# First transposes issued between the row loads, 24 tiles of row statistics moved to the second and third batch, slot rows fetched a slot earlier

## The chip, the cores and the metric

The kernel runs on one core of a Trainium2 chip. The metric is the device time of one execution in microseconds (us); lower is better. The engines are TensorE (PE, with its weight loads listed apart as PEld), VectorE (DVE), ScalarE (ACT), GpSimd (POOL) and SyncE (SP, which here only issues DMAs and waits).

## What is computed

Two layers over x [16, 256, 256] with a context ctx of the same shape and a mask of keys:

```python
x = x + _L0_xattn_ref(ctx_1024, ctx_1024, _layernorm(x, axis=-1), mask, W_out, b_out)   # 16 heads of 16
x = x + _L0_ffn_ref(_layernorm(x, axis=-1), w1, b1, w2, b2)                             # quantised MLP
x = x + _L1_xattn_ref(_layernorm(x, axis=-1), ctx_1024, ctx_1024, Wq, bq, ...)          # autocorrelation
x = x + _L1_ffn_ref(_layernorm(x, axis=-1), Wfc_s, ..., Wr, Wfc, bfc, Wproj, bproj)     # 8 experts, top 2, and a shared one
```

The first line is a softmax attention: the layer-normed x are the queries, ctx is both keys and values, masked scores are -1e20, and the result is projected by W_out. The layer norm of a row needs its mean and variance ("row statistics"). The last line routes each of the 4096 rows to 2 of 8 experts and adds the gated results to the output of the shared expert.

## The kernel before

The 4096 rows are 32 tiles of 128; tile T sits in `X[:, T, :]`, two tiles (`NQ`) are one batch. The program runs four blocks: `attention`, `quant_mlp`, `autocorrelation`, `moe`. In each, every engine has its own program text in hand-written order, and semaphores tie them together.

**attention** works in phases `B` from -2 to 16 (`PHASES`), each of 8 steps `hp` (a pair of heads). In phase B, PE computes the scores of batch B+1 (`scores`, L569), which DVE reduces to row maxima with the mask added (`take_max`, L747, four 256-column calls in a step), and the transposed scores of batch B (`scoresT`, L582), which ACT exponentiates (`exponent`, L479). PE then weighs the values (`weigh`, L615), transposes and projects. PE may write the scores of the next step only when DVE has read those of the step before (`s_red`), and `scoresT` of a step only when the exponent two steps back is done (`s_exp`).

Ahead of that, batch b+2 is prepared in phase B = b. DVE reads the mask (`see_mask`). POOL combines the rows' scale with it (`set_live`), ACT normalises the two tiles (`normal_rows`, L460), and POOL splits the result in f16 parts (`split_q`, L394 to L397) and the context rows too (`split_k`, L383 to L386). Then SP turns them by DMA transposes of 128 rows each (`turn_k` L297, `turn_q` L307, `turn_mask` L317). POOL also adds the projection's bias to the rows of x (`add_bias`, L402), which waits for all of x, `bo_bc` and `woT` (`s_x[2]` at 80), copies the values (`values`), and cuts expert weights for the last block in f16 parts (`cut_piece`, L151 to L155, two pieces in a phase). The first `scores` of all, in phase -1, wait for `turn_k(0)` and `turn_q(0)`.

Row statistics are taken in three groups of tiles (`GROUPS`): 2, 6 and 24 tiles. For each group DVE runs `measure` (one `bn_stats` a tile, L693) and `norm_begin` (6 small steps), ACT the square root (`std`, L453), DVE `norm_end` (6 more). Group 2, the 24 tiles from batch 4 on, is first used by `set_live(4)`, in phase 2. Exponent and square root are in different tables of ACT, so a switch is an ACT_TABLE_LOAD.

**moe** runs the shared expert over 16 chunks and then 39 slots of 256 rows (every sixth, from slot 2 on, has 128). A tick of PE is: transpose the rows of slot s+1 (`rows_T`, L2028), first layer of slot s (L2043), second layer of slot s-1 (L2056). SP fetches for each slot the first weights (`first_weights`, L1835, 1 MB, once the hidden layer of slot s-2 has left PSUM), the second weights (`second_weights`, L1842, 1 MB, once DVE has taken the output of slot s-2) and the rows (`slot_rows`, L1851, once PE, POOL and DVE have used those of slot s-2, since there are two row buffers). All three stand in one queue. POOL copies the rows' owners (`own`, L1900) and adds the gated output rows to the output in DRAM (`add_rows`, L1908), one slot after the other, each waiting for the landing of the one before.

## Time and profile before

| | us |
|---|---|
| median of 3 runs | 1292.04 (1291.15 to 1297.92) |
| the profiled execution | 1290.28 |
| its span, first to last instruction | 1288.5 |
| attention, from the first score to batch 2's first scores | 30.0 to 87.3 |
| slots of the last block, on PE | 874 to 1271 |

PE is busy for 88% of the span, DVE for 65%, ACT and POOL for 45% each. The mean granted TensorE clock is 0.961 of full speed. A row of the timeline view gives start, duration, engine and line, and in brackets how long the engine had been idle and what ended it. SPq rows are DMA issues: their duration is that of the issue, not of the transfer.

### The profile page before, as it was taken

The numbers are of one execution on the slowest core, as the hardware profiler recorded it, in microseconds if no ns is written. First come the engines' busy times: TensorE is split into PE (matmuls) and PEld (weight loads), VectorE is DVE, ScalarE is ACT, GpSimd is POOL, SyncE is SP. The second block draws the span as 40 slices with busy tenths as digits, with TensorE's granted clock in tenths as the row PEclk, the third lists the DMA queues.
The fourth block names the chain that finished last, engine by engine and source line by source line (L and its number), as shares of the span: only waits on it lengthen the run. The fifth ranks groups of instructions, "written<-read, shape, count | busy, mean of one in ns | idle before, by whom it ended". The sixth has DMA issues, their size and how long they took to land. (4 is left out here: it accounts for less than half of the span.)

```text
span 1288.5 us, 27824 instructions
## 1 busy us (share of the span) xinstructions
PE 1138.7 (88%) x9970; PEld 862.2 (67%) x9970; DVE 836.7 (65%) x2627; ACT 587.5 (46%) x1065; POOL 576.0 (45%) x644
## 2 busy tenths in 40 slices
PE   0699999998677979979569999998999999999996
PEld 0144444444323658867458888887898888988895
DVE  4999999998697742237364686555656565666663
ACT  1288888887544723235028433333333343433331
POOL 6487778786540047966000006660233323333333
PEclk9999999999699989999677999999999999999998
DMA  9478877875420035620449033326989899888884
GB/s 287 84 175 164 179 170 169 163 163 176 132 66 2 1 98 172 201 116 1 132 135 239 4 112 112 113 101 219 274 246 282 252 273 266 270 262 257 270 260 99
DMA packets 180758, 215.66 MB, mean 167 GB/s; under 512 B 91936, under 2 KB 163488, under 8 KB 168112
## 3 DMA queue, kind: packets, MB, share of 16 engines
q1 hardware_dynamic: 167360, 197.42, 52.9%
q0 software_dynamic: 13296, 16.92, 6.7%
q8 instruction: 58, 0.95, 0.3%
q14 instruction: 44, 0.36, 0.1%
HBM read 143.86 MB, written 50.38 MB: 151 GB/s over the span
## 5 line engine op out<-in xcount | busy, mean ns | idle before, releaser
L2056 PE MATMUL banks<-moe_w,moe_hT 128*128 128x256 f16 x2472 | 278.5, 273 | 0.0
L2056 PEld LDWEIGHTS banks<-moe_w,moe_hT 128*128 128x128 f16 x2472 | 241.6, 98 | 27.9
L1965 ACT ACTIVATE moe_hf<-banks,moe_b 128x256 f32<-128x256 f32 (+1 forms) x440 | 178.5, 457 | 170.2 <-PE banks L2043 169.2
L1908 POOL DMA_INDIRECT out_x<-moe_y,slot_owner x71 | 116.9, 1646 | 270.7 <-DMA out_x<-moe_y,slot_owner 163.8
L747 DVE CUSTOM_DVE_ANT_0 masked<-banks,mask_bias 128x256 f32<-128x256 f32 x512 | 185.9, 420 | 30.7 <-PE banks L569 27.0
L2043 PE MATMUL banks<-moe_rT,moe_w 128*128 128x256 f16 (+1 forms) x1872 | 194.3, 264 | 0.0
L2043 PEld LDWEIGHTS banks<-moe_rT,moe_w 128*128 128x128 f16 x1872 | 170.4, 98 | 17.9
L479 ACT ACTIVATE probsT<-banks 128x1024 f32<-128x1024 f32 x128 | 130.7, 1021 | 48.8 <-PE banks L600 48.8
L2177 DVE TENSOR_TENSOR moe_hT<-moe_hf,moe_hT 128x512 f16<-128x512 f32 (+1 forms) x220 | 145.4, 661 | 7.6
L569 PE MATMUL banks<-kT,qT 48*128 48x256 f16 x512 | 92.2, 285 | 48.5 <-DMA qT<-q_split 30.0
L1894 POOL DMA_INDIRECT slots_x<-moe_xn,pos x64 | 64.1, 1002 | 140.7 <-DVE pos L2255 109.6
L2175 DVE CAST moe_hT<-moe_hf 128x512 f16<-128x512 f32 (+1 forms) x220 | 91.4, 415 | 45.2 <-ACT moe_hf L1965 43.2
L151 POOL TENSOR_SCALAR half_rows<-half_rows 128x512 f32<-128x512 f32 x72 | 107.5, 1493 | 11.5 <-DMA moe_halves<-half_parts 5.9
L569 PEld LDWEIGHTS banks<-kT,qT 48*128 48x128 f16 x512 | 34.2, 96 | 106.7 <-issue 54.8
L1949 ACT ACTIVATE moe_rT<-banks 128x512 f16<-128x512 f32 (+1 forms) x39 | 21.8, 559 | 183.2 <-PE banks L2028 183.2
L2300 DVE SCALAR_TENSOR_TENSOR moe_y<-banks,moe_b 128x512 f32<-128x512 f32 (+1 forms) x39 | 25.1, 644 | 112.2 <-PE banks L2056 104.9
L2043 PE MATMUL banks<-moe_xnT,moe_w 128*128 128x256 f16 x768 | 90.5, 277 | 0.0
L155 POOL TENSOR_TENSOR half_parts<-half_rows,half_parts 128x512 f16<-128x512 f32 x72 | 83.9, 1165 | 6.2
L582 PE MATMUL banks<-qmT,kT 64*128 64x256 f16 x512 | 86.1, 279 | 0.0
L2043 PEld LDWEIGHTS banks<-moe_xnT,moe_w 128*128 128x128 f16 x768 | 76.4, 100 | 9.7
L1085 PE MATMUL banks<-xqT,w1T 128*128 128x512 bf16 x256 | 67.3, 393 | 12.5 <-ACT hf L1044 5.7
L615 PE MATMUL banks<-probsT,v_ones 128*32 128x256 f32 x1024 | 70.2, 393 | 0.3 <-ACT qmT L486 0.3
(336 smaller groups left out, 1783.1 us busy)
## 6 DMA issues: line engine op xcount, KB each, us to landing
moe_w<-moe_halves SPq DMA_DIRECT2D x80, 1024.0 KB, 5.1
moe_halves<-half_parts SPq DMA_DIRECT2D x18, 1024.0 KB, 6.2
slots_x<-empty_row SPq DMA_DIRECT2D x1, 9230.0 KB, 47.5
moe_rows<-slots_x SPq DMA_DIRECT2D x32, 260.0 KB, 6.5
half_rows<-in_L_ffn_Wfc SPq DMA_DIRECT2D x8, 1024.0 KB, 8.5
half_rows<-in_L_ffn_Wproj SPq DMA_DIRECT2D x8, 1024.0 KB, 8.4
moe_b<-in_L_ffn_bproj SPq DMA_DIRECT2D x39, 128.0 KB, 6.2
ctx_rows<-in_ctx SPq DMA_DIRECT2D x16, 256.0 KB, 3.1
```

The costliest lines, as they stand in the source:

```text
L151: pool.tensor_scalar(rows[:, cols], rows[:, cols], WSCALE, None, ALU.mult).then_inc(w["cut"], 1)
L155: pool.tensor_tensor(parts[:, 1, cols], rows[:, cols], parts[:, 0, cols], ALU.subtract).then_inc(w["cut"], 1)
L479: act.activation(probsT[n % EXPS][:].rearrange("p j k q -> p (j k q)"), psum_t[n % 2][:], ACT.Exp, scale=SCALE).then_inc(s_exp, 1)
L569: ins = pe.matmul(psum_s[:, at:at + S], qT[b % 2][rows, hp, t * P:(t + 1) * P], kT[b % 3][rows, hp, :], start=(t == 0), stop=(t == NQ - 1))
L582: pe.matmul(psum_t[n % 2][:, at:at + S], kT[b % 3][rows, hp, k * P:(k + 1) * P], qmT[b % 2][rows, hp, :], start=(k == 0), stop=False)
L747: ins = v.tensor_tensor_reduce(masked[2 * j + t][:], psum_s[:, at:at + S], mask_bias[b % 2][:, t, :], 1.0 / SHIFT, -3e38, ALU.add, ALU.max ...
L1908: pool.indirect_dma_start(out=out_rows, out_offset=bass.IndirectOffsetOnAxis(ap=owner[:, s, t:t + 1], axis=0), in_=y[s % 2][:, t, :], in_o ...
L1965: ins = act.activation(hf[p][:, j, 0:width], src, ACT.Gelu_apprx_tanh, bias=b1[buffer][:, j:j + 1], scale=1.0 / WSCALE)
L2043: ins = pe.matmul(banks[jp // 2][:, at:at + width], w1[buffer][:, w, k, j * P:(j + 1) * P], moving(x, k), start=(k == 0 and (w, x) == PART ...
L2056: ins = pe.matmul(OUT[p][:, t * D:(t + 1) * D], hT[p][:, x, j, t * P:(t + 1) * P], w2[buffer][:, w, j, :], start=(j == 0 and (w, x) == PAR ...
L2175: v.tensor_copy(hT[p][:, 0, at, 0:width], hf[p][:, at, 0:width]).then_inc(e_hh, 1)
L2177: v.tensor_tensor(hT[p][:, 1, at, 0:width], hf[p][:, at, 0:width], hT[p][:, 0, at, 0:width], ALU.subtract).then_inc(e_hl, 1)
```

## The change

It has three parts. In the start of `attention`, SP loads the second mask ahead of the second context rows, and issues the transposes of batch 0 between the three loads of the last 24 tiles of x instead of behind them and the first two expert halves; POOL splits the context rows of batch 1 earlier (before `add_bias(0)`) and moves its first `cut_piece` behind `split_q(1)`. The 24 `bn_stats` of group 2 move from the 8 steps of phase -1 (3 in each) to the first 12 steps from phase 0 on (2 in each); `norm_begin(2)` follows step 11, the root comes on ACT in step 12, after the exponent and `set_mask(3)` and before the exponent of step 13, and `norm_end(2)` after step 14. In `moe`, `slot_rows` is issued one iteration earlier (for slot s+3 instead of s+2), and `own` with it.

```diff
+        MEASURED_IN = 12
 ...
+            load_mask(1)
             load_ctx(1)
-            load_mask(1)
-            for c in range(3):
+
+            def load_rows(c):
                 w = (c1 - c0) // 3
                 sp.dma_start(X[:, c0 + c * w:...], ...).then_inc(s_x[2], 16)
+
+            load_rows(0)
+            turn_k(0)
+            load_rows(1)
+            turn_q(0)
+            load_rows(2)
 ...
-                if real(B + 2):
+                if real(B + 2) and B > -2:
                     turn_k(B + 2)
                     turn_q(B + 2)
 ...
@@ gpsimd
-                if B >= -1:
+                if B >= 0:
                     cut_piece(pool, g.cut, 2 * (B + 1))
 ...
                 if B == -2:
+                    split_k(B + 3)
 ...
+                if B == -1:
+                    cut_piece(pool, g.cut, 0)
                 if real(B + 2):
                     add_bias(B + 2)
 ...
-                if real(B + 3):
+                if real(B + 3) and B > -2:
                     split_k(B + 3)
 ...
@@ scalar
                 if B == 0:
-                    std(2)
                     act.preload_act_table(ACT.Exp)
 ...
+                    if HP * B + hp == MEASURED_IN:
+                        std(2)
+                        act.preload_act_table(ACT.Exp)
 ...
@@ vector
-                    if B == 0 and hp == 1:
-                        norm_end(2)
 ...
-                    if B == -1:
+                    step = HP * B + hp
+                    if 0 <= step < MEASURED_IN:
                         v.wait_ge(s_x[2], 80)
                         lo, hi = GROUPS[2]
-                        measure(lo + (hi - lo) * hp // HP, lo + (hi - lo) * (hp + 1) // HP)
-                    if B == -1 and hp == HP - 1:
+                        measure(lo + (hi - lo) * step // MEASURED_IN, lo + (hi - lo) * (step + 1) // MEASURED_IN)
+                    if step == MEASURED_IN - 1:
                         norm_begin(2)
+                    if step == MEASURED_IN + 2:
+                        norm_end(2)
 ...
@@ moe, sync
+            slot_rows(0, 2)
             for s in range(NSLOT - 1):
+                if s + 3 < NSLOT:
+                    slot_rows(*divmod(s + 3, PERIOD))
                 if s + 2 < NSLOT:
-                    slot_rows(*divmod(s + 2, PERIOD))
                     first_weights(*divmod(s + 2, PERIOD))
 ...
@@ moe, gpsimd
+            own(2)
             for s in range(NSLOT):
-                if s + 2 < NSLOT:
-                    own(s + 2)
+                if s + 3 < NSLOT:
+                    own(s + 3)
                 add_rows(s)
```

SP at the start of `attention`, before (`w1q_rounded` holds the split context rows of even batches, `w2q_rounded` of odd ones):

```order
L327 DMA ident<-in_ident 128x128
L283 DMA ctx_rows<-in_ctx 128x2x256
L288 DMA mask_int<-in_mask_Bx1xSxS_ik 128x2x256
L330 DMA X<-in_x 128x6x256
L283 DMA ctx_rows<-in_ctx 128x2x256
L288 DMA mask_int<-in_mask_Bx1xSxS_ik 128x2x256
L335 DMA X<-in_x 128x8x256 x3
L336 DMA bo_bc<-in_L_xattn_b_out 128x256
L337 DMA woT<-in_wo0T 128x2x256
L132 DMA half_rows<-in_L_ffn_Wfc 128x2x1024
L132 DMA half_rows<-in_L_ffn_Wproj 128x8x256
L297 DMA_TRANSPOSE kT<-w1q_rounded 128x8x128 x2
```

and SP at the same place now:

```order
L331 DMA X<-in_x 128x6x256
L289 DMA mask_int<-in_mask_Bx1xSxS_ik 128x2x256
L284 DMA ctx_rows<-in_ctx 128x2x256
L337 DMA X<-in_x 128x8x256
L298 DMA_TRANSPOSE kT<-w1q_rounded 128x8x128 x2
L337 DMA X<-in_x 128x8x256
L308 DMA_TRANSPOSE qT<-q_split 128x8x128 x2
L337 DMA X<-in_x 128x8x256
L344 DMA bo_bc<-in_L_xattn_b_out 128x256
L345 DMA woT<-in_wo0T 128x2x256
L132 DMA half_rows<-in_L_ffn_Wfc 128x2x1024
L132 DMA half_rows<-in_L_ffn_Wproj 128x8x256
```

The transposes of batch 0 have moved ahead of two row loads (`turn_k`) or one (`turn_q`), the bias, `woT` and both halves.

ACT in phase 1, from the exponents of its third and fourth step on, before:

```order
L479 ACTIVATE probsT<-banks 128x1024 x2
L492 ACTIVATE oT_raw<-banks 128x256
L479 ACTIVATE probsT<-banks 128x1024
L471 ACTIVATE mask_bias<-mask_all,row_live 128x256 x2
L479 ACTIVATE probsT<-banks 128x1024
L492 ACTIVATE oT_raw<-banks 128x256
L508 ACTIVATE oT<-banks 128x512
```

and there now:

```order
L490 ACTIVATE probsT<-banks 128x1024 x2
L503 ACTIVATE oT_raw<-banks 128x256
L490 ACTIVATE probsT<-banks 128x1024
L482 ACTIVATE mask_bias<-mask_all,row_live 128x256 x2
L464 ACT_TABLE_LOAD
L464 ACTIVATE ln_std<-ln_b 128x24
L544 ACT_TABLE_LOAD
L490 ACTIVATE probsT<-banks 128x1024
L503 ACTIVATE oT_raw<-banks 128x256
L519 ACTIVATE oT<-banks 128x512
```

The root and two table loads stand between two exponents. Before, the root and one load stood ahead of the first exponent of all; that one load has stayed there.

SP in `moe`, one iteration, before (the numbered weight tiles are the two buffers):

```order
L1842 DMA moe_w_1<-moe_halves 128x4096
L1843 ISA
L1843 DMA moe_b_1<-in_L_ffn_bproj 128x256
L1851 DMA moe_rows<-slots_x 128x2x260
L1829 TENSOR_LOAD slot_e
L1829 ISA x2
L1835 ISA
L1835 DMA moe_w_1<-moe_halves 128x4096
```

and one iteration now:

```order
L1856 DMA moe_w_1<-moe_halves 128x4096
L1857 ISA
L1857 DMA moe_b_1<-in_L_ffn_bproj 128x256
L1865 DMA moe_rows<-slots_x 128x260
L1843 TENSOR_LOAD slot_e
L1843 ISA x2
L1849 ISA
L1849 DMA moe_w_1<-moe_halves 128x4096
```

The rows keep their place between second and first weights, but they are those of the slot after: the short one (128x260) stands here one iteration earlier than it did.

## Rows read from the trace of the kernel before

**Rows 1.** Timeline, 0 to 31 us: DMA issues of SP, POOL's part steps, the first scores.

```profile
4.74 6.34 SPq L335 DMA_DIRECT2D X<-in_x  x3
7.58 0.80 POOL L386 COPY w1q_rounded<-w1q_rounded 128x512 f16<-128x512 f16 x1
13.20 0.60 POOL L397 COPY q_split<-q_split 128x512 f16<-128x512 f16 x1
15.50 9.81 SPq L297 DMA_TRANSPOSE kT<-w1q_rounded  x2
20.12 1.40 POOL L402 TENSOR_TENSOR X<-X,bo_bc 128x256 f32<-128x256 f32 x2 [5.38 <-DMA woT<-in_wo0T]
30.01 0.61 PE L569 MATMUL banks<-kT,qT 48*128 48x256 f16 x4 [30.01 <-DMA qT<-q_split]
```

**Rows 2.** Issue to landing: first two L335 loads, first `kT` and `qT` transposes.

```profile
L335 SPq DMA_DIRECT2D X<-in_x x2: 877/1580/2283, 4.7 to 5.7; - x2
...
DMA to landing us min/median/max: 8.8/9.7/10.6
...
L297 SPq DMA_TRANSPOSE kT<-w1q_rounded x2: 2665/4882/7099, 15.5 to 22.6; - x2
...
DMA to landing us min/median/max: 4.7/7.8/10.9
...
L307 SPq DMA_TRANSPOSE qT<-q_split x4: 1285/1320/1337, 25.4 to 35.3; - x4
...
DMA to landing us min/median/max: 3.2/3.3/3.3
```

**Rows 3.** Timeline of phase -1 and its end: DVE, PE and ACT.

```profile
30.73 0.42 DVE L747 CUSTOM_DVE_ANT_0 masked<-banks,mask_bias 128x256 f32<-128x256 f32 x1 [13.69 <-PE banks L569]
31.08 0.42 DVE L747 CUSTOM_DVE_ANT_0 masked<-banks,mask_bias 128x256 f32<-128x256 f32 x1
31.57 1.29 PE L569 MATMUL banks<-kT,qT 48*128 48x256 f16 x4 [0.95 <-DVE row_max L747]
32.12 1.08 DVE L693 BATCH_NORM_STATS2 stats<-X 128x6 f32<-128x256 f32 x3
52.03 0.65 DVE L706 TENSOR_TENSOR ln_a<-stats 128x24 f32<-128x24 f32 x1
53.84 0.42 DVE L747 CUSTOM_DVE_ANT_0 masked<-banks,mask_bias 128x256 f32<-128x256 f32 x1
54.07 1.28 ACT L516 ACT_TABLE_LOAD   x1
55.37 1.02 ACT L479 ACTIVATE probsT<-banks 128x1024 f32<-128x1024 f32 x1
```

**Rows 4.** Windows: start:end, us; busy (count) of PE, PEld, DVE, ACT, POOL; clock, DMA.

```profile
30.00:53.84 23.84, 12.85 (x60) 3.90 (x60) 22.66 (x103) 1.03 (x2) 11.98 (x17) 1.00 0.56 114
53.84:70.30 16.46, 13.49 (x142) 4.67 (x142) 13.92 (x74) 13.74 (x18) 8.36 (x10) 1.00 0.31 73
70.30:87.27 16.97, 16.49 (x208) 7.86 (x204) 15.55 (x82) 13.96 (x20) 13.71 (x19) 1.00 0.72 145
87.27:103.80 16.53, 16.25 (x200) 8.25 (x196) 15.34 (x81) 13.57 (x19) 13.75 (x20) 1.00 0.85 208
```

**Rows 5.** Waits, PE in 870 to 1288 us: us in total, times, longest.

```profile
PE banks L2028 <- DMA moe_rows<-slots_x: 8.4, 10, 2.8
```

**Rows 6.** Timeline of PE: the first two `rows_T` that waited for rows.

```profile
874.37 0.63 PE L2028 MATMUL banks<-ident,moe_rows 128*128 128x128 f32 x4 [0.86 <-DMA moe_rows<-slots_x]
885.15 0.65 PE L2028 MATMUL banks<-ident,moe_rows 128*128 128x128 f32 x2 [2.78 <-DMA moe_rows<-slots_x]
```

**Rows 7.** Timeline behind a short slot: rows' issue, PE's wait, POOL's next `add_rows`.

```profile
1084.27 0.38 SPq L1851 DMA_DIRECT2D moe_rows<-slots_x  x1
1091.64 0.66 PE L2028 MATMUL banks<-ident,moe_rows 128*128 128x128 f32 x4 [1.12 <-DMA moe_rows<-slots_x]
1096.46 1.94 POOL L1908 DMA_INDIRECT out_x<-moe_y,slot_owner  x1 [6.66 <-DMA out_x<-moe_y,slot_owner]
```

## The prediction

> **What bounds the kernel now.** I read the timeline from the start, since the first two parts of the change act there. PE's first scores come at 30.01, after 30 us of nothing, and what ended the wait is the landing of `qT` [rows 1]. The f16 parts that these transposes need were there long before: those of k at 8.4 (7.58 + 0.80), those of q at 13.8 (13.20 + 0.60) [rows 1]. They waited in SP's queue: the issue of the two `kT` transposes takes from 15.5 to 25.3 [rows 1], because 3 MB of x, the weights and two halves of 1 MB are ahead of them on the same queue, and an X load lands 8.8 to 10.6 us after its issue [rows 2]. With nothing in the way a transpose lands 3.2 to 3.3 us after its issue [rows 2].
>
> Next comes phase -1, from 30.0 to 53.84. DVE is busy for 22.66 of 23.84 us and PE for 12.85 [rows 4]: DVE is the bound, and a good part of it is the 24 statistics. In the next two phases both are near full: 16.46 us with PE 13.49 and DVE 13.92, 16.97 us with PE 16.49 and DVE 15.55. From phase 2 on a phase is 16.53 us with PE at 16.25 and DVE at 15.34 [rows 4]: PE bounds, and DVE has 1.2 us to spare.
>
> In the last block PE waits for slot rows 10 times, 8.4 us in all [rows 5]. Two of these are in the first slots [rows 6], the others stand behind the short slots, as at 1091.64 [rows 7]. The rows are issued at 1084.27 and PE wants them at 1090.5 (1091.64 - 1.12) [rows 7]: a short tick and a DMA of 7.3 us don't fit.
>
> **Part 1, the first transposes.** Up to the first X load (4.74 to 5.6) SP's issues take what they took, in another order. Then it waits for `split_k(0)`, 8.4. The two `kT` issue by about 11 (1.3 us each); ahead of them on the queue is only the first X load, which lands at 13.5 (4.7 + 8.8) [rows 2]. Loads of 1 MB land 2.7 us apart (4.7 + 8.8 and 5.7 + 10.6) [rows 2]. A transpose behind another lands 0.9 us after it (15.5 + 10.9 and 22.6 + 4.7) [rows 2]. So `kT` 15.3, the second X load 18.0, `qT` 19.8. The first scores come at **20.0 instead of 30.0**. The floor is `qT` without company: 13.9 + 1.3 + 3.2 = 18.4; the ceiling, if the transposes' issue is held up by the loads as it is at 15.5, is about 24.
>
> What is queued behind the new waits on SP: the second and third X load, the bias, `woT`, halves, the mask of batch 2. `woT` lands four transposes later, 20.1 + 3.6 = 23.7; `add_bias(0)` on POOL waits for it, and behind that stand `set_live(1)` (0.6 us), ACT's `normal_rows(1)` (1.1) and `split_q(1)` (2.4): 23.7 + 1.4 + 0.6 + 1.1 + 2.4 is 29.2, so `turn_q(1)` issues at about 30 and lands at 34, the swapped mask of batch 0 at 36. Here the earlier `split_k(1)` and the later `cut_piece(0)` (3.3 us) pay: neither stands in this chain any more. Before, the same chain ended at 37 with phase 0 at 53.84, and it hid; now it is next in line.
>
> **Part 2, the statistics.** Three take 1.08 us [rows 3], 24 take 8.6; `norm_begin` takes 1.8 (52.03 to 53.84) [rows 3], `norm_end` 1.4. Phase -1 loses 8.6 + 1.8. Its DVE time from 30.73 to 53.84 is 23.1 us; 12.7 is left. But the statistics also covered PE: after a pair of maxima is read PE refills in 0.6 us at half clock, and with the signals on both sides the pair is ready 0.78 after, while DVE's other pair takes 0.70 (two calls 0.35 apart [rows 3]). That leaves 0.16 a step, 1.3 in 8 steps: 14.0. DVE would begin phase 0 at 20.7 + 14.0 = 34.7; with the mask and `qT(1)` at 34 to 36 I take **35.3 instead of 53.84**.
>
> The work comes back in phases 0 and 1. Phase 0 gets 16 statistics, 5.7 us, and loses `norm_end`, 1.4. If the idle time of both engines took it in, the phase would be DVE's 13.92 + 4.3 = 18.2; if none did, 16.46 + 4.3 = 20.8. PE writes one step ahead at most and its steps are uneven, so I take the upper one. Phase 1 gets 8 statistics, `norm_begin` and `norm_end`, 2.9 + 1.8 + 1.4 = 6.1: between 15.55 + 6.1 = 21.7 and 16.97 + 6.1 = 23.1; in it two steps hold 2 to 2.5 us of extra DVE work at once, and I take 22.3. Then ACT: the root's switch adds two table loads of 1.28 us [rows 3], and the phase before had one ahead of the first exponent, which stays. Behind them wait the exponent of step 13, the copies of `oT_raw` and `oT`. PE needs that exponent two steps on, and ACT has 3 us a phase to spare (13.57 of 16.53) [rows 4], but not in these steps; the cost is 0 to 2.8, I take 1.0. Phase 2 begins at 35.3 + 20.8 + 22.3 + 1.0 = 79.4 instead of 87.27: **7.9 us less**. The ends: 18.5 + 0.7 + 14.0 + 18.2 + 21.7 = 73.1 (14 less), and 24.7 + 14.0 + 20.8 + 23.1 + 2.8 = 85.4 (1.9 less). After that PE bounds as before; the first user of the late root, `set_live(4)`, wants it at phase 2, some 4 us behind `norm_end(2)`, and ACT's normalisation of batch 4 a step later, with a phase to go to its scores.
>
> On the table loads row and rule differ. The row has the load from 54.07 to 55.35 and the exponent at 55.37 [rows 3], so a switch is 1.3 us. The Trainium skill ("ScalarE: Activation LUTs", What ACT_TABLE_LOAD costs) gives 1.28 us and a drain of 1.38 for every switch. By that two loads would be 5.3 us, and if all that is over 2.6 reached PE, the result would be 2.7 later.
>
> **Part 3, the slot rows.** No work is added. Rows of slot s+3 are issued when PE has transposed those of s+1, a whole tick earlier. Nothing on SP waits longer for it: its conditions are met at the start of tick s, and the first weights behind it wait for the hidden layer of slot s, half a tick later. `own(s+3)` now stands ahead of `add_rows(s)`, with its rows landed in tick s and `add_rows(s)` not due before tick s+2. The first two waits, 0.9 and 2.8 [rows 6], stay: there the rows of slots 0 and 2 are issued where they were. The other eight go: 8.4 - 3.7 = **4.7 us** [rows 5]. Bounds: 0, if another late transfer takes their place, and 4.7, since no more of PE's waits is for rows.
>
> **The sum.** 7.9 + 4.7 = 12.6. From the profiled execution, 1290.28, that is 1277.7. The median of the runs is 1.8 above that execution, so **1279.4**. The other blocks only shift.
>
> **Rivals.** *The start is eaten up.* The DVE work is moved, not removed, and if the transposes do queue behind the loads and neither phase hides a statistic, the attention gains 1.9; with part 3 the median is 1292.0 - 6.6 = 1285.4. For it speaks DVE at 85 and 92% in phases 0 and 1 (13.92 of 16.46, 15.55 of 16.97) [rows 4]; against it that parts are ready at 8.4 and 13.8.
>
> *The rows don't pay.* POOL's `add_rows` chain waits for landings, 6.66 us at a time [rows 7], each for the one before. If faster ticks run into it, it holds `moe_y`, DVE holds the second weights, and PE's waits come back elsewhere: 1292.0 - 7.9 = 1284.1. Against it: no wait of PE for weights or for output stands among its waits now, only those for rows [rows 5].
>
> *The clock stays low (slower).* Matmuls of phase -1 and the start of phase 0 run at half speed, 1.2 GHz: phase 0 holds less PE work than phase 1 in nearly the same time [rows 4]. With DVE as the bound PE has gaps in every step of phases 0 and 1. If the full clock came only with phase 3, PE's 16.25 [rows 4] would be between once and twice that; I estimate 1.6 times, 26 us, so 78 for three phases against 43.1 + 16.5 in the forecast: +18.4, which turns 12.6 less into 5.8 more, 1297.8. It decides in the third such phase; two cost 8.9. Against it: at half clock PE's own work fills the steps, so its gaps close.
>
> *It does less than it says.* The order is fixed by hand, so the moves are certain; both gains near their lower ends, 1.9 and 0, give 1290.1.
>
> **How the numbers follow.** Forecast 0.63 (1272 to 1286 as its own spread, by the bounds of the two phases), start eaten up 0.14, rows don't pay 0.10, both small 0.08 (1288 to 1292), clock 0.05. The range must leave no more than 0.2 out: 1272 to 1289. A measurement tells about 0.5%, 6.5 us, from no change, so faster means under 1285.6: nearly all of the forecast, half of the next two: 0.73. Within 0.5%: 0.20, slower 0.07.
>
> **What would show it.** First scores at 18.5 to 24 us, waiting for `qT`; DVE's maxima of phase -1 in steps of about 1.6 us; first exponents of phases 0, 1, 2 at about 37, 57, 81 instead of 55.4, 71.5, 87.5; no gap over 2 us on PE behind the root in step 12; `rows_T` without a wait from 900 us on. I'm wrong if phases 0 and 1 take more than 23 us each, if the first scores come after 25, or if PE's waits for rows give way to waits for weights.

## The result and the profile after

The changed kernel takes 1281.62 us (median of 10 runs, 1275.96 to 1284.37), against 1291.16 (10 runs, 1287.57 to 1297.92) for the kernel before: ratio 0.9923, 95% interval 0.9905 to 0.9941, or 9.9 us less (7.6 to 12.3). The forecast was 1279.4, 12.6 us less than the 1292.0 then known. The profiled execution took 1284.37 us, the longest of the ten, its span 1282.6, at a mean granted clock of 0.958.

The start of the timeline answers to [rows 1]. Columns are start, duration, engine and line; SPq rows are issues.

```profile
8.95 4.99 SPq L298 DMA_TRANSPOSE kT<-w1q_rounded  x2
13.99 0.59 SPq L337 DMA_DIRECT2D X<-in_x  x1
14.63 6.19 SPq L308 DMA_TRANSPOSE qT<-q_split  x2
20.86 0.58 SPq L337 DMA_DIRECT2D X<-in_x  x1
...
22.11 0.43 SPq L345 DMA_DIRECT2D woT<-in_wo0T  x1
...
22.99 0.62 PE L582 MATMUL banks<-kT,qT 48*128 48x256 f16 x4 [22.99 <-DMA qT<-q_split]
```

The first scores come at 22.99 instead of 30.01, not at 20.0. The pair of `kT` issues takes 4.99 us where two free issues take 2.6 (1.3 each), so the second X load is issued at 13.99; the second pair takes 6.19, the third load is issued at 20.86, and `woT` at 22.11. What leads to phase 0 is this, SP, POOL, DVE and PE in the same view:

```profile
23.98 2.68 SPq L289 DMA_DIRECT2D mask_int<-in_mask_Bx1xSxS_ik  x1
...
26.70 4.85 SPq L318 DMA_TRANSPOSE mask_biasT<-mask_bias  x2
...
29.64 1.41 POOL L410 TENSOR_TENSOR X<-X,bo_bc 128x256 f32<-128x256 f32 x2 [11.81 <-DMA woT<-in_wo0T]
...
31.68 4.37 SPq L298 DMA_TRANSPOSE kT<-w2q_rounded  x2
...
34.66 0.61 POOL L405 COPY q_split<-q_split 128x512 f16<-128x512 f16 x1
...
35.88 0.43 DVE L742 TENSOR_SCALAR mask_all<-mask_int 128x512 bf16<-128x512 int32 x1 [1.37 <-DMA mask_int<-in_mask_Bx1xSxS_ik]
...
36.14 2.65 SPq L308 DMA_TRANSPOSE qT<-q_split  x2
...
40.73 0.37 PE L582 MATMUL banks<-kT,qT 48*128 48x256 f16 x1 [5.56 <-DMA qT<-q_split]
```

POOL stands idle for 11.81 us until `woT` lands at 29.6, and the parts of q of batch 1 are ready at 35.3. But SP is not free for their transposes before 36.05: from 20.86 on its issues follow each other with at most 0.13 us between them, the mask's pair takes 4.85 us and that of k 4.37. So it is SP's own queue that comes last, by 0.8 us, and not the chain from `woT`. PE waits 5.56 us for these transposes, and phase 0 begins at 40.7 instead of the forecast's 35.3. DVE was through with phase -1 at 39.1, so the feed holds up phase 0 by 1.6 us; the rest of the 5.4 is in DVE's own chain too, which began 3.0 us late with the scores and waited 1.37 us for the mask of batch 2.

Windows of the phases answer to [rows 4] (start:end, us; busy and count of PE, PEld, DVE, ACT, POOL; clock, DMA share, GB/s):

```profile
22.99:41.50 18.51, 10.58 (x48) 3.21 (x48) 13.95 (x73) 4.20 (x6) 10.89 (x15) 1.00 1.06 273
41.50:60.50 19.00, 15.23 (x160) 5.88 (x156) 18.00 (x83) 12.64 (x17) 15.78 (x22) 0.91 0.61 129
60.50:85.00 24.50, 20.20 (x192) 8.83 (x192) 20.64 (x98) 16.70 (x22) 16.99 (x25) 0.79 0.61 162
85.00:101.60 16.60, 16.16 (x194) 8.18 (x196) 15.39 (x82) 13.17 (x18) 11.13 (x14) 1.00 0.54 108
```

DVE now does 18.00 us of work in phase 0 and 20.64 in phase 1. Phase 1, 24.50 us long, is the dear one: full for neither engine, at a clock of 0.79, where [rows 4] shows 16.97 us at 1.00. Phase 2 is as before.

The slots, PE's waits from 870 us on (total, times, longest), answer to [rows 5]:

```profile
PE banks L2045 <- DMA moe_rows<-slots_x: 4.4, 2, 3.8
PE banks L2045 <- DVE moe_rT L2301: 1.5, 1, 1.5
```

Ten waits for rows have become two, at 876.7 (3.8) and 888.1 (0.6); no wait for weights or output has come up. From the first to the last `rows_T` it is 372.0 us (876.7 to 1248.7) instead of 380.2 (874.4 to 1254.6).

### The profile page after: what moved, and what is told of

Its sections match the earlier page's. It is cut to its first block and busy times, and to the rows that moved or that the text cites. A ratio compares the mean times of both kernels' runs of the same rounds, so it can differ in the third digit from the quotient of the medians.

```text
span 1282.6 us, 27814 instructions
## 1 busy us (share of the span) xinstructions
PE 1139.6 (89%) x9959; PEld 864.0 (67%) x9970; DVE 837.2 (65%) x2627; ACT 591.2 (46%) x1067; POOL 575.0 (45%) x644
## 5 line engine op out<-in xcount | busy, mean ns | idle before, releaser
L2060 PEld LDWEIGHTS banks<-moe_rT,moe_w 128*128 128x128 f16 x1872 | 170.9, 99 | 18.3
L490 ACT ACTIVATE probsT<-banks 128x1024 f32<-128x1024 f32 x128 | 130.6, 1021 | 62.3 <-PE banks L613 62.0
L582 PE MATMUL banks<-kT,qT 48*128 48x256 f16 x512 | 92.7, 287 | 44.5 <-DMA qT<-q_split 28.5
L582 PEld LDWEIGHTS banks<-kT,qT 48*128 48x128 f16 x512 | 35.0, 96 | 102.1 <-issue 55.9
L628 PE MATMUL banks<-probsT,v_ones 128*32 128x256 f32 x1024 | 72.8, 404 | 0.0
## 6 DMA issues: line engine op xcount, KB each, us to landing
slots_x<-empty_row SPq DMA_DIRECT2D x1, 9230.0 KB, 43.5
```

Of the source, the lines that this page charges most:

```text
L490: act.activation(probsT[n % EXPS][:].rearrange("p j k q -> p (j k q)"), psum_t[n % 2][:], ACT.Exp, scale=SCALE).then_inc(s_exp, 1)
L582: ins = pe.matmul(psum_s[:, at:at + S], qT[b % 2][rows, hp, t * P:(t + 1) * P], kT[b % 3][rows, hp, :], start=(t == 0), stop=(t == NQ - 1))
L2060: ins = pe.matmul(banks[jp // 2][:, at:at + width], w1[buffer][:, w, k, j * P:(j + 1) * P], moving(x, k), start=(k == 0 and (w, x) == PART ...
```

## The experiments

Each difference is given against runs of the kernel before on the same chip: the ratio times 1290 us. All kernels compute everything unless it is said otherwise. Starts of the first exponent of a phase are from ACT's rows of each timeline; "phase 0" and "phase 1" are the distances between them. The last column is how long the granted clock stood at 1.2 GHz in phase 1 (in the windows view of the changed kernel it is the 0.79 of 24.5 us). It doesn't show all of the slow time at the start: in the kernel before the granted clock reads 1.00 there [rows 4], but PE's 48x256 matmuls take 0.39 to 0.42 us up to 62.7 and 0.28 behind that. The same durations stand in the changed kernel up to 44.8. In phase 1 such durations come with a granted 1.2 GHz.

| kernel | ratio (95%) | us against before | first scores | exponents of phases 0, 1, 2 | phase 0 | phase 1 | half clock in phase 1 |
|---|---|---|---|---|---|---|---|
| before | | | 30.0 | 55.4, 71.5, 87.5 | 16.1 | 16.1 | 0 |
| after | 0.9923 (0.9905 to 0.9941) | -9.9 | 23.0 | 42.4, 61.3, 85.9 | 18.9 | 24.6 | 10.2 |
| e1 | 0.9953 (0.9936 to 0.9970) | -6.1 | 30.5 | 55.9, 72.2, 88.2 | 16.3 | 16.1 | 0 |
| e2 | 0.9987 (0.9976 to 0.9998) | -1.7 | 21.1 | 51.8, 68.1, 84.1 | 16.3 | 16.1 | 0 |
| e3 | 0.9993 (0.9979 to 1.0007) | -0.9 | 30.0 | 45.2, 62.8, 87.6 | 17.6 | 24.8 | 10.2 |
| e4 | 0.9972 (0.9956 to 0.9987) | -3.6 | 22.6 | 42.3, 61.1, 84.1 | 18.8 | 23.0 | 3.4 |
| e5 | 0.9937 (0.9916 to 0.9959) | -8.1 | 21.6 | 36.9, 63.0, 87.6 | 26.1 | 24.5 | 6.8 |
| e6 | 0.9921 (0.9899 to 0.9943) | -10.2 | 21.7 | 42.0, 61.2, 86.0 | 19.2 | 24.8 | 10.2 |
| e7 | 0.9900 (0.9877 to 0.9924) | -12.9 | 22.5 | 47.5, 65.6, 81.7 | 18.1 | 16.1 | 0 |
| e8 | 0.9892 (0.9869 to 0.9915) | -13.9 | 21.3 | 44.5, 62.3, 78.4 | 17.8 | 16.1 | 0 |
| e9 | 0.9932 (0.9916 to 0.9948) | -8.8 | 22.8 | 38.1, 62.1, 87.0 | 24.0 | 24.9 | 11.2 |
| e10 | 0.9947 (0.9926 to 0.9967) | -6.8 | 23.7 | 43.6, 63.1, 89.7 | 19.6 | 26.6 | 10.2 |
| e11 | 0.9895 (0.9879 to 0.9911) | -13.5 | 23.4 | 46.3, 64.6, 80.9 | 18.3 | 16.3 | 0 |
| e12 | 0.9887 (0.9870 to 0.9905) | -14.6 | 22.6 | 39.6, 64.2, 80.2 | 24.6 | 16.1 | 0 |

**e1, part 3 alone.** The slot rows of the change on the kernel before, and `own` one slot earlier as well (not shown in this cut).

```diff
@@ moe, sync
+            slot_rows(0, 2)
             for s in range(NSLOT - 1):
+                if s + 3 < NSLOT:
+                    slot_rows(*divmod(s + 3, PERIOD))
                 if s + 2 < NSLOT:
-                    slot_rows(*divmod(s + 2, PERIOD))
```

> The kernel before with part 3 alone (slot rows and owner copies one slot earlier). Theory A, the gain is the slot rows': PE's waits for slot rows fall from 8.4 us to under 4, the stretch of the slots from 380 us to 372, and the whole is 7 to 10 us faster, as much as the changed kernel. Theory B, the forecast: 4.7 us faster from here, the rest from the attention.

6.1 us less (3.9 to 8.3). PE's waits for rows fell from 8.4 [rows 5] to

```profile
PE banks L2031 <- DMA moe_rows<-slots_x: 3.3, 2, 1.8
```

and the stretch of slots from 380.2 to 371.8 us. All PE gaps in that stretch fell from 9.2 to 3.0; another 1.7 is the third tick, 12.4 us before and 10.8 here, in which before's clock was at half for 3.4 us. That tick is 13.7 us in e6 and 12.1 in e8, which have the slot rows of e1 as well, so this 1.7 varies from run to run and is not the change's. The total lies between the two theories (7 to 10, and 4.7), and its interval reaches both.

**e2, part 1 alone.** The statistics of before, three a step in phase -1, with the new transposes.

```diff
+            load_rows(0)
+            turn_k(0)
+            load_rows(1)
+            turn_q(0)
+            load_rows(2)
```

> The kernel before with part 1 alone (transposes of batch 0 between the row loads, context split earlier, first piece later); the statistics stay in phase -1. First scores at 23 us instead of 30. Theory A: qT of batch 1 lands at about 40.6 here too, but phase -1 with its 24 statistics takes 23 us, so DVE enters phase 0 at 23.7 + 23.1 = 46.8 and not at 53.8: 5 to 7 us faster than before. Theory B (the start is eaten up later, by the preparation of batch 1 and 2 on POOL and SP): under 2 us faster.

1.7 us less (0.3 to 3.1), although the scores came 9 us earlier. DVE's second step of phase -1 shows why:

```profile
27.74 1.08 DVE L704 BATCH_NORM_STATS2 stats<-X 128x6 f32<-128x256 f32 x3 [4.49 <-DMA woT<-in_wo0T]
```

The statistics wait for all five loads that share a semaphore, the last of them `woT`, which they don't read. In this profile the exponent of phase 2 comes 3.4 us earlier, more than the total says. The total is theory B's, but not its reason: the exponent of phase 0 comes only 3.6 us earlier, so most of the lead is gone within phase -1.

**e3, part 2 alone.** The transposes and slot rows of before, the statistics, root and norm steps of the change (the cut shows the statistics).

```diff
-                    if B == -1:
+                    step = HP * B + hp
+                    if 0 <= step < MEASURED_IN:
                         v.wait_ge(s_x[2], 80)
```

> The kernel before with part 2 alone (24 statistics in the first 12 steps from phase 0 on, root between two exponents). Phase -1 falls from 23.8 us to about 15 and phase 0 starts at 45 instead of 53.8, but phases 0 and 1 take 19 and 24.5 us as in the changed kernel instead of 16.5 and 17. Theory A: 10.4 us of DVE work leave, 10 come back with a half-clock stretch and the table switch, so the whole is within 2 us of before, or slower by 1 to 2. Theory B, the forecast's arithmetic: about 2 us faster.

0.9 us less, which can't be told from none (2.7 less to 0.9 more). Phase 0 began 10.2 us earlier, and at phase 2 the exponent stood at 87.6, where before has 87.5: phases 0 and 1 had given all of it back.

**e4, parts 1 and 2.** The changed kernel with the slots of before, e1's diff the other way round.

> The changed kernel without part 3 (slot rows as before). Theory A: exponents of phase 2 begin at 86 instead of 87.5 us, and the whole is 0 to 2 us faster than before. Theory B, the forecast: 7.9 us faster.

3.6 us less. With e1's 6.1 that is 9.7 of the measured 9.9, so the two places add up, and the attention brought less than half of the 7.9 that I had forecast. The total (1.7 to 5.7) lies above theory A's 0 to 2, if only just, and well short of B's 7.9. Up to the last block this is the changed kernel's own program, and yet phase 1 took 23.0 us here with 3.4 of half clock, and 24.6 there with 10.2.

**e5, the feed of batch 1.** On the changed kernel:

```diff
@@ sync
-            for n in range(2):
-                load_half(sp, d, w, n)
+            load_mask(2)
             for B in PHASES:
 ...
                     swap_mask(B + 1)
+                if B == -1:
+                    for n in range(2):
+                        load_half(sp, d, w, n)
@@ gpsimd
                 if B == -1:
+                    add_bias(0)      # was ahead of set_live(1)
                     cut_piece(pool, g.cut, 0)
```

> The changed kernel with another order of the start: on SP the load of the mask of batch 2 and the transposes for batches 0 and 1 stand ahead of the two halves of 1 MB, and POOL adds the bias of batch 0 (which waits for the output weights) behind the parts of q of batch 1 instead of ahead. Nothing is left out. Theory A (phase 0 waits for the transposes of q of batch 1, which are held up by the halves and the output weights): after has 40.73 us for the first scores of phase 0 with a wait of 5.56 us for qT, so here these scores stand at 35 to 37, the first exponent of phase 0 at 37 to 39 instead of 42.4, and the total falls by 3 to 5 us, to about 1277 by medians. Theory B (the work of the first phases bounds the start, not the feed): phase 0 begins earlier but phases 0 and 1 take longer by the same, the first exponent of phase 2 stays at 84 to 86 and the total stays within 1 us of after, 1281.6.

The feed came as early as the forecast had put it: the first exponent of phase 0 at 36.9 (forecast 37). The total didn't follow. In phase 0 ACT and PE stood still:

```profile
50.06 1.09 ACT L474 ACTIVATE q_rows<-X,live_shift,live_scale 128x256 f32<-128x256 f32 x2 [9.66 <-POOL live_shift L434]
...
52.20 0.37 PE L598 MATMUL banks<-qmT,kT 64*128 64x256 f16 x1 [8.34 <-ACT probsT L493]
```

POOL's `set_live(2)` stands behind the first cut pieces, which wait for the halves that I had moved back (landing at 38.8 and 42.0); ACT's `normal_rows(2)` waits for it, and the exponents wait behind that. Theory B has the better of it in the result. Its reason, the work of the first phases, is not what held phase 0 here.

**e6, without the table switch.** `std(2)` in step 12 is a copy in place of a root and the preload behind it is gone; the rows from batch 4 on are scaled by the variance instead of its root.

```diff
                     if HP * B + hp == MEASURED_IN:
-                        std(2)
-                        act.preload_act_table(ACT.Exp)
+                        std(2, ACT.Copy)
```

> The changed kernel with the root of the last 24 tiles as a copy and without the exponent's table loaded behind it, so that the two table loads of step 12 are gone (the rows of batches 4 and up are normalised with the variance in place of its root). The prediction put the loads at 1.0 us, with bounds 0 and 2.8. Theory A (only the part of the loads that ACT has no slack for reaches PE): the gap of PE of 1.81 us and DVE's wait of 1.62 us at 74.8 to 79.7 in after go down to the 0.6 us that other steps have, and the total is 1 to 1.5 us below after. Theory B (phases 0 and 1 are bound by DVE's own work, and the loads hide under it): the total is within 0.5 us of after. By the Trainium skill (ScalarE: Activation LUTs, What ACT_TABLE_LOAD costs) a switch drains ScalarE for a further 1.38 us, which by that rule would make it 2.7 us more.

10.2 us less than before, the changed kernel 9.9: the switch costs nothing that these runs can tell. Phase 1 took 24.8 us, and the gap of PE in the step of `norm_begin` was as wide without the loads:

```profile
74.47 0.39 PE L581 MATMUL banks<-kT,qT 48*128 48x256 f16 x1 [2.27 <-DVE row_max L759]
```

**e7, statistics where DVE is idle.** On the changed kernel, with `std(2)` and `norm_end(2)` back where they were before:

```diff
@@ load_rows(c)
-                sp.dma_start(X[:, c0 + c * w:...], ...).then_inc(s_x[2], 16)
+                sp.dma_start(X[:, c0 + c * w:...], ...).then_inc(s_xr[c], 16)
 ...
                     if B == -1 and hp == 0:
                         norm_end(1)
+                        v.wait_ge(s_xr[0], 16)
+                        measure(8, 16)
 ...
+                    if B == -1:
+                        if hp % 4 == 0:
+                            v.wait_ge(s_xr[1 + hp // 4], 16)
+                        measure(16 + 2 * hp, 18 + 2 * hp)
+                    if B == -1 and hp == HP - 1:
+                        norm_begin(2)
```

> The changed kernel with its statistics in other places: 8 tiles measured right ahead of the first maxima, where DVE stands idle from 18.3 to 23.7 us in after, the other 16 tiles two a step in phase -1, root and the end of the normalisation ahead of phase 0 as in the kernel before, and so no table switch in step 12. Each of the three X loads has a semaphore of its own, so that no statistic waits for the output weights. Transposes and slot rows are those of the changed kernel. Theory A (DVE's work fills the time from the first scores to phase 2, and idle time ahead of them is free): the first exponent of phase 0 comes at 42 to 45, a phase then takes 16 to 18 us, the first exponent of phase 2 comes at 77 to 80 instead of 85.9 and the total falls by 5 to 8 us, to 1274 to 1277. Theory B (phases 0 and 1 are slow for another reason, such as the clock or the transfers of the start): they take 43 us here as well, the exponent of phase 2 stays at 85 or later and the total stays at 1281 to 1284.

12.9 us less than before, about 3 better than the changed kernel (the intervals overlap). The exponent of phase 2 comes 4.2 us earlier than there. Eight statistics run in the idle time of DVE ahead of the first maxima, and phases 0 and 1 are shorter, 18.1 and 16.1 us instead of 18.9 and 24.6:

```profile
17.77 2.71 DVE L708 BATCH_NORM_STATS2 stats<-X 128x6 f32<-128x256 f32 x8
```

```profile
22.00:46.50 24.50, 12.86 (x60) 3.93 (x60) 22.95 (x97) 3.46 (x7) 16.06 (x24) 1.00 0.93 228
46.50:64.80 18.30, 14.51 (x144) 5.04 (x144) 15.52 (x73) 13.45 (x18) 13.10 (x18) 1.00 0.55 99
64.80:80.90 16.10, 15.59 (x192) 7.54 (x194) 14.78 (x77) 13.27 (x19) 11.87 (x15) 1.00 0.66 133
```

DVE's busy time from the first scores to phase 2 is 53.3 us (22.95 + 15.52 + 14.78), in the changed kernel 52.6 (13.95 + 18.00 + 20.64), though eight statistics (2.7 us) fewer are in it: POOL held up its norm steps (last section), and `norm_begin` took 3.3 us (42.58 to 45.91) instead of 1.6. Even so these stretches take 58.9 us here and 62.0 there. In phase -1 the work closes up: DVE is busy for 22.95 of 24.50. The result has theory A's direction and not its size: the exponents of phases 0 and 2 were to come at 42 to 45 and 77 to 80 and came at 47.5 and 81.7, and it wanted 5 to 8 us from the changed kernel.

**e8, both.** e7's statistics with e5's order.

> The last two layouts together: the statistics as in e7 and the order of the start as in e5. Theory A (one bound at a time: with 16 statistics in phase -1 DVE reaches phase 0 at about 42, later than the transposes of q of batch 1 in either order): within 1.5 us of e7. Theory B (the feed is what counts in both): 3 to 5 us below e7.

13.9 less, 1 better than e7 and not to be told from it, as theory A says: DVE, not the feed, sets the start of phase 0. In the profiles the exponent of phase 2 is 3.3 us earlier than e7's. Of that 1.1 is the first scores. Another 1.8 lies between first scores and first maxima of phase 0, and there DVE's busy time is less by as much (20.55 us against 22.39) and POOL's is 8.05 against 15.50; the last section has what POOL does to DVE's steps.

**e9, e5 mended.** On e5, `set_live(2)` ahead of `add_bias(0)` in phase -1.

```diff
@@ gpsimd
-                if real(B + 2):
+                if real(B + 2) and B != 0:
                     set_live(B + 2)
 ...
                 if B == -1:
+                    set_live(2)
                     add_bias(0)
```

> e5 once more, with POOL's set_live(2) ahead of the bias of batch 0 and of the first two cut pieces, instead of behind them. In e5 ACT waited 9.66 us for it at 50.06 with the exponents of phase 0 queued behind, since the pieces waited for the halves that had been moved back. Nothing is left out. Theory A (the feed of batch 1 cost after 4 to 5 us, and e5 only traded it for this wait): no wait of ACT over 2 us in phase 0, first exponents of phases 0, 1, 2 at 37, 56, 80.5 instead of 42.4, 61.3, 85.9 in after, total 4 to 5 us below after's. Theory B (something else holds phases 0 and 1 to where they are, and the 5.5 us come back anyway): the exponent of phase 2 stays at 84 or later and the total within 1.5 us of after's.

The wait of ACT is gone, the exponent of phase 2 still comes at 87.0. POOL and PE:

```profile
38.88 1.50 POOL L151 TENSOR_SCALAR half_rows<-half_rows 128x512 f32<-128x512 f32 x1 [1.36 <-DMA half_rows<-in_L_ffn_Wfc]
...
55.25 0.61 POOL L407 COPY q_split<-q_split 128x512 f16<-128x512 f16 x1
...
60.38 0.37 PE L586 MATMUL banks<-kT,qT 48*128 48x256 f16 x1 [5.96 <-DMA qT<-q_split]
```

From 38.9 to 60.6 POOL has no idle time at all; three cut pieces of 3.3 us stand ahead of `split_q(2)`, which ends at 55.9 instead of 52.7 in the changed kernel, and PE waits for its transposes. The changed kernel has the same three pieces ahead, but starts them at 35.24; here the first waits until 38.88 for a half that was moved back. The wait for the feed of batch 1 had become one for the feed of batch 2. The result is theory B's.

**e10, the statistics in 8 steps.** On the changed kernel:

```diff
-        MEASURED_IN = 12
+        MEASURED_IN = 8
```

> The changed kernel with its 24 statistics in the 8 steps of phase 0, three a step, and the root with its two table loads and norm_begin and norm_end in steps 7 to 10. Nothing is left out. This parts the price of the statistics from that of the small norm steps. Theory A (a phase takes its time of before plus what its added DVE work is, plus about 0.25 us for each us of half clock in it): phase 0 takes 16.1 + 8.6 - 1.4 + 1.5 (most of norm_begin) + half clock, 25 to 26, phase 1 takes 16.0 + 1.6 to 3 = 18 to 19, together about 43.5 as in after, total within 1.5 us of after. Theory B (the small steps are what costs, and statistics hide to a good part): phase 0 takes 20 to 22, phase 1 21 or more. Theory C (the statistics cost more where three stand together): the sum is 46 or more.

By the exponents the sum, 46.2 us, is theory C's and the split theory B's, 19.6 and 26.6. But three of the statistics (62.91) and `norm_begin` (64.02 to 65.99) stand behind the maxima that the exponent at 63.15 waits for, so they fall in "phase 1". By DVE's own first maxima (42.55, 66.03, 89.49; before: 53.84, 71.28, 87.27) the phases are 23.5 and 23.5 us. Phase 0 grew by 6.0 us for 9.2 of added work (8.6 - 1.4 + 2.0), and phase 1 by 7.5, with nothing but `norm_end` added (3.5 us). So part of the statistics hides, as theory B says. What makes phase 1 longer than its added work isn't parted here: in it DVE waits for PE (up to 2.01 us at a time), at a granted clock of 0.78. DVE's `norm_end` and POOL in the same time:

```profile
73.33 0.67 DVE L731 TENSOR_TENSOR ln_a<-rstd 128x24 f32<-128x24 f32 x1
74.02 0.52 DVE L732 TENSOR_TENSOR ln_a<-ln_a,ln_b 128x24 f32<-128x24 f32 x1
74.57 0.65 DVE L733 TENSOR_SCALAR ln_a<-ln_a 128x24 f32<-128x24 f32 x1
75.25 0.65 DVE L734 TENSOR_TENSOR rstd<-rstd,ln_a 128x24 f32<-128x24 f32 x1
```

```profile
72.78 1.16 POOL L404 TENSOR_TENSOR q_split<-q_rows,q_split 128x512 f16<-128x512 f32 x1
73.89 0.61 POOL L405 COPY q_split<-q_split 128x512 f16<-128x512 f16 x1
74.46 1.40 POOL L410 TENSOR_TENSOR X<-X,bo_bc 128x256 f32<-128x256 f32 x2
```

Steps that take 0.18 us in the changed kernel (rows in the last section) take 0.52 to 0.67 here, and each ends with one of POOL's: 74.00 with 73.94, 74.54 with 74.50, 75.22 and 75.90 within 0.06 us of the ends of its two instructions (1.40 us together from 74.46). `norm_end` took 3.5 us (73.00 to 76.48) instead of 1.4.

**e11, 12 tiles ahead.** On e8:

```diff
                         measure(8, 16)
+                        v.wait_ge(s_xr[1], 16)
+                        measure(16, 20)
 ...
-                        measure(16 + 2 * hp, 18 + 2 * hp)
+                        measure(20 + 12 * hp // HP, 20 + 12 * (hp + 1) // HP)
```

> e8 with 12 instead of 8 tiles measured ahead of the first maxima and 12 instead of 16 in phase -1. In e8 DVE stood idle for 1.46 us between the 8 statistics and the first maxima, and DVE bounds all from there to phase 0. Theory A: the four statistics move into the idle time, the first exponent of phase 0 comes 1.3 us earlier than in e8 (43.2), and so does all behind it: total 1.3 below e8. Theory B (the start of phase 0 hangs on the feed): no change against e8.

13.5 less, the same as e8. From the first scores to the first exponent it is 23.0 us instead of 23.2, not the 1.3 less that theory A wants: the 4 statistics are 1.4 us less in phase -1, but `norm_begin` took 3.4 (41.35 to 44.78) instead of 2.3, again beside POOL.

**e12, spread.** 12 tiles ahead as in e11, 8 in phase -1 and 4 in phase 0, the root with two table loads in step 4 of phase 0.

```diff
                     if B == -1:
-                        measure(20 + 12 * hp // HP, 20 + 12 * (hp + 1) // HP)
-                    if B == -1 and hp == HP - 1:
+                        measure(20 + hp, 21 + hp)
+                    if B == 0 and hp < 4:
+                        measure(28 + hp, 29 + hp)
+                    if B == 0 and hp == 3:
                         norm_begin(2)
+                    if B == 0 and hp == 6:
+                        norm_end(2)
```

> e8 with 12 tiles ahead of the first maxima, one tile a step in phase -1 (8), one a step in the first four steps of phase 0 (4), norm_begin in step 3, the root with two table loads in step 4 and norm_end in step 6. Nothing is left out. Theory A (PE-bound phases take in about 1.5 us of DVE work each at no cost, as phase 0 of after did): the first exponent of phase 0 comes at 39 to 40 and that of phase 2 at 75 to 76, 2 to 3 us before e8's 78.4; total 2 to 3 below e8. Theory B (every us of DVE work at the start costs one, wherever it stands, and in phase 0 the clock falls as well): exponent of phase 2 at 77 or later, total at e8's or above.

14.6 less, the best median (1274.56), though not apart from e7, e8 and e11. Phase 0 began at 39.6, 5 us before e8's, and took 24.6 us, with e5's wait in it:

```profile
49.40 1.09 ACT L478 ACTIVATE q_rows<-X,live_shift,live_scale 128x256 f32<-128x256 f32 x2 [6.32 <-POOL live_shift L438]
...
51.54 0.37 PE L602 MATMUL banks<-qmT,kT 64*128 64x256 f16 x1 [5.33 <-ACT probsT L497]
```

So its exponent of phase 2, 80.2, is no earlier than e8's 78.4, which is what theory B says of the exponent. e9's `set_live(2)` together with this layout was not tried.

## Why the prediction was right, and where it was not

**Where it had it right.** Faster, by two gains that add up, 9.9 against 12.6 us; 1281.62 lies in the range. The wait that remained, for `turn_q(1)`, was named too, but not what held it up. The total is closer than its parts, and that is luck: the attention gave 3.6 instead of 7.9 (e4), less than half, and the slot rows 6.1 instead of 4.7 (e1).

**Part 1: the queue.** I took "`kT` 15.3, the second X load 18.0, `qT` 19.8". `kT` landed at 15.9, but the issue of its pair took 5.0 us and not 2.6, so the second load was issued at 14.0, where the sum had all loads running 2.7 us apart as if issued early. It landed at 20.9, and with `qT` the same happened again. What was mis-sized is the issue of a transpose behind a load that is still running: up to 4 us where the pair on a free queue needs 1.3 each. I had this as the ceiling for the scores ("if the transposes' issue is held up by the loads", about 24), and didn't carry it to `woT`, 29.6 against 23.7, nor to the transposes behind it. The pairs of the mask and of k of batch 1 take 4.85 and 4.37 us here, where the kernel before has 2.46 and 2.62 (at 28.72 and 31.30), so `turn_q(1)` was issued at 36.14 and not at about 30. With `woT` on time SP would still not have been free before 36.05, if the issues had taken what they took; e4 and e6 have the same order of events (parts ready at 35.1 and 34.8, k's pair issued to 35.9 and 35.4). Phase 0 moved from 35.3 to 40.7, 5.4 us later. DVE's own chain to it was 4.4 late (39.1 against 34.7): the scores by 3.0, the mask's landing by 1.4.

**Phase -1.** DVE's plain steps are 1.48 us apart (the scores that PE refills behind them start at 26.03, 27.50, 28.98), against the 1.6 forecast. From the first maxima, 23.7, to the end of the phase, 39.1, it is 15.4 us; without the wait for the mask that is the 14.0 of the sum. This term held.

**Phases 0 and 1.** Together 43.5 us by the exponents and 44.3 by DVE's first maxima (41.35, 61.74, 85.68); the forecast was 20.8 + 22.3, and 1.0 for ACT, 44.1. So the sum held, but its parts were wrong in both directions. The mark between the phases that it took from [rows 4], 70.30, is PE's first scores; DVE's first maxima of phase 1 start at 71.28, which makes the two phases of before 17.4 and 16.0 us. Phase 0 took 20.4, which is 3.0 more for 4.3 us of added work, where I had all 4.3: part of the statistics hides. Phase 1 took 23.9, which is 8.0 more for my 6.1, and beyond the upper bound of 23.1. The 1.0 for ACT is not in it (e6). DVE's busy time there grew by 5.1 us (20.64 against 15.55 in the windows shown); the rest is DVE waiting for PE. Rows of the changed kernel at both clocks:

```profile
64.36 1.94 PE L628 MATMUL banks<-probsT,v_ones 128*32 128x256 f32 x16
...
66.87 0.42 DVE L760 CUSTOM_DVE_ANT_0 masked<-banks,mask_bias 128x256 f32<-128x256 f32 x1 [0.98 <-PE banks L582]
...
69.67 1.07 PE L628 MATMUL banks<-probsT,v_ones 128*32 128x256 f32 x16
...
74.83 0.28 PE L582 MATMUL banks<-kT,qT 48*128 48x256 f16 x1 [1.81 <-DVE row_max L760]
...
79.70 0.42 DVE L760 CUSTOM_DVE_ANT_0 masked<-banks,mask_bias 128x256 f32<-128x256 f32 x1 [1.62 <-PE banks L582]
```

The granted clock is at 1.2 GHz from 61.9 to 68.7; PE then waits 1.81 us through `norm_begin`, and it is there again from 75.5 to 78.9. `weigh` takes 1.94 us instead of 1.07, and DVE waits for PE in turn. I read this as a lump of DVE work that is paid in full, with PE's catching up on top; no run parts the two. This is the rival of the low clock, in small and over by phase 2: it did not become slower than before. In phase 1 all seven kernels with moved statistics or norm steps there have half clock, 3.4 to 11.2 us, and take 23.0 to 26.6 us; the seven others have none and take 16.1 to 16.3. Of those with 8 statistics in it, the one with 3.4 us takes 23.0 and the four with 10.2 or more take 24.6 to 24.9, which would put a phase at full clock at 22.2, an estimate. The changed kernel and e4, one program up to there, differ by 1.6 us for 6.8 of half clock. But e5, with 6.8 us, has 24.5, where this line has 23.9, so how much of phase 1 is the clock is not settled.

**The net of part 2.** With the feed at the forecast's time (e5, e9) nothing was gained, since POOL came next: it has no idle time from 38.9 to 60.6 in e9, having waited for the first half up to there. I had priced the cut pieces as out of the chain of batch 1 and not looked at what they do to the chain of batch 2. e5 and e9 also move the halves back, so they show this bound with the halves late; where it would lie with the halves early isn't shown. The term of 7.9 us measured 3.6 (e4). That feed, POOL and clock would all have had to give way for it is an inference; no run has all three.

**The table switch.** The two loads stand in the changed kernel's rows, with no time behind them:

```profile
74.31 1.28 ACT L464 ACT_TABLE_LOAD   x1
75.61 0.22 ACT L464 ACTIVATE ln_std<-ln_b 128x24 f32<-128x24 f32 x1
75.85 1.28 ACT L544 ACT_TABLE_LOAD   x1
77.14 1.03 ACT L490 ACTIVATE probsT<-banks 128x1024 f32<-128x1024 f32 x1
```

Without them the total is the same within the interval (e6). By the Trainium skill ("ScalarE: Activation LUTs", What ACT_TABLE_LOAD costs) a drain of 1.38 us would belong to each. The exponent starts 0.01 us after the second load, so here the trace doesn't agree.

**Part 3.** Forecast 4.7, measured 6.1 (3.9 to 8.3), and the eight waits it named are gone. The two first ones, 3.7 by the forecast, are 3.3 in e1 and 4.4 in the changed kernel. "`rows_T` without a wait from 900 on" held.

## What to carry to other kernels

Before work is moved off an engine that bounds the start, look for idle time of that same engine ahead of the start: eight statistics fitted there, and with only this done and the group's norm steps left in place, the same kernel was about 3 us better by the medians than with the work pushed into the following phases (the intervals overlap; its phase 2 began 4.2 us earlier). A semaphore shared by loads of different users makes each wait for the last one (4.49 us of DVE in e2). When transposes are put among running loads, add up the issuing queue itself: what stands far behind them is late as well. And when a wait is taken away, follow the next batch's chain on every engine, POOL's too, not the present batch's alone.

## What the runs showed of the hardware

DVE's norm steps are held by most of POOL's instructions until that one's end, as e10's rows show. The same steps in the changed kernel with POOL waiting:

```profile
82.48 0.18 DVE L731 TENSOR_TENSOR ln_a<-rstd 128x24 f32<-128x24 f32 x1
82.69 0.18 DVE L732 TENSOR_TENSOR ln_a<-ln_a,ln_b 128x24 f32<-128x24 f32 x1
```

```profile
83.67 0.20 POOL L431 TENSOR_TENSOR live_scale<-rstd,row_live 128x2 f32<-128x2 f32 x1 [1.13 <-issue]
```

The maxima, which read PSUM, aren't held: in e10 one takes its usual 0.42 us in the middle of POOL's instruction.

```profile
75.83 1.49 POOL L151 TENSOR_SCALAR half_rows<-half_rows 128x512 f32<-128x512 f32 x1
```

```profile
76.51 0.42 DVE L760 CUSTOM_DVE_ANT_0 masked<-banks,mask_bias 128x256 f32<-128x256 f32 x1
```

That instruction, the TENSOR_SCALAR of a cut piece, is the exception among POOL's. `norm_begin` in e10 meets it as well:

```profile
63.79 1.50 POOL L151 TENSOR_SCALAR half_rows<-half_rows 128x512 f32<-128x512 f32 x1
```

```profile
64.49 0.20 DVE L720 TENSOR_TENSOR nmr<-stats 128x24 f32<-128x24 f32 x1
```

This step and the three behind it take 0.18 to 0.20 us in the middle of it. Only a step that meets its beginning is held, and then to about 0.65 us after its start: to 64.45 and 76.48 in e10 and 44.57 in e11, where it starts at 63.79, 75.83 and 43.92. Why, the runs don't show. The Trainium skill ("SBUF — State Buffer", SBUF: two separate sides) says that VectorE and GpSimd share a pair of ports which is locked for a whole instruction. The trace agrees for POOL's casts, copies and two-input steps, with up to 0.49 us more a step and 2 us more for six in e10, and up to 1.0 us more for a step in e7 (1.20 instead of 0.20, at 43.72); for this TENSOR_SCALAR it doesn't.

A transpose issued behind running loads takes long to issue: 4.99 and 6.19 us for pairs that take 2.65 where fewer loads run (36.14), and 2.46 to 2.69 in the kernel before from 25.4 on. And the time of the first scores, with the same transposes in the same order, lay between 21.1 and 23.7 us in the profiles of 11 kernels; single profiles tell the start to no better than that.
